# One transformer tower on one core: the first attention's mixing with 128 stationary columns, three divisions, and key slots and a bias moved to other engines

## The reference, cut to what matters

```python
q, k, v = (qkv[:, :, 0], qkv[:, :, 1], qkv[:, :, 2])     # 8 heads, hd = 8
...
scores = jnp.einsum('bhwqd,bhwkd->bhwqk', q, k) * scale
attn = jax.nn.softmax(scores, axis=-1)
out = jnp.einsum('bhwqk,bhwkd->bhwqd', attn, v)          # the mixing
out = out.transpose(0, 2, 3, 1, 4).reshape(B, N, D)
return jnp.einsum('bnd,ed->bne', out, proj_w) + proj_b
...
for n, T in enumerate(NUM_SCALES):                        # second attention
    bias = bias + beta[n] * jnp.cos(two_pi * absdiff / T)
```

## Time and profile before

| | |
|---|---|
| median of 3 runs | 130.06 us (129.52 to 131.12) |
| the profiled execution | 130.09 us |
| its span, first to last instruction | 128.3 us |
| outside the span | 1.8 us |
| instructions | 2347 |
| VectorE, ScalarE, GpSimd busy | 85.2, 62.8, 16.9 us |

### The profile page before, as it was taken

How to read it: one execution, slowest core, us unless ns; L and a number is a source line. 1 busy time by engine, 2 the same in 40 slices (tenths; PEclk the granted TensorE clock), 3 DMA queues, 4 the chain that set the end, 5 groups by cost and what they waited for, 6 DMA issues and landing times.

```text
span 128.3 us, 2347 instructions
## 1 busy us (share of the span) xinstructions
PE 114.1 (89%) x912; PEld 75.3 (59%) x919; DVE 85.2 (66%) x181; ACT 62.8 (49%) x124; POOL 16.9 (13%) x40
## 2 busy tenths in 40 slices
PE   5999999969999989999999996999999999799630
PEld 2334564737687764795686884878768772224330
DVE  0000599799996354558798644487599949999960
ACT  4000668965132175655853647573575646443040
POOL 7300009300000000000022003270013400000000
PEclk9999999999999999999999999999999999999997
DMA  4999980000000000000000000000000000000003
GB/s 156 331 391 432 418 331 2 0 0 0 5 0 3 5 0 0 3 0 5 0 0 0 5 0 0 5 0 0 0 0 0 0 0 3 0 0 5 0 0 82
DMA packets 2682, 6.99 MB, mean 55 GB/s; under 512 B 1264, under 2 KB 1392, under 8 KB 2544
## 3 DMA queue, kind: packets, MB, share of 16 engines
q1 hardware_dynamic: 2672, 6.86, 14.1%
HBM read 6.59 MB, written 0.26 MB: 53 GB/s over the span
## 4 chain that ended last, share of the span: by engine, by line
PE 59%; DVE 17%; DMA 7%; issue 6%; ACT 4%; POOL 2%; SPq 2%; POOLq 1%; ACTq 0%
DMA shared_x<-x_dram 7%; PE PS L395 5%; PE PS L627 5%; PE PS L628 5%; PE PS L309 4%; PE PS L511 3%; PE PS L381 3%; PE PS L635 3%; PE PS L298 3%; PE PS L372 3%; PE PS L497 3%; DVE shared_x L1338 3%; DVE shared_h L1268 2%; PE PS L405 2%; PE PS L317 2%
## 5 line engine op out<-in xcount | busy, mean ns | idle before, releaser
L1268 DVE TENSOR_TENSOR shared_h<-PS,shared_f 128x512 f32<-128x512 f32 x22 | 14.9, 682 | 5.3 <-ACT shared_f L880 5.2
L627 PE MATMUL PS<-xf,up_hi 128*128 128x512 f32 x44 | 17.8, 404 | 0.3 <-DVE shared_h L1268 0.3
L628 PE MATMUL PS<-xf,up_lo 128*128 128x512 f32 x44 | 17.4, 396 | 0.0
L880 ACT ACTIVATE shared_f<-PS 128x512 f32<-128x512 f32 x22 | 12.9, 595 | 7.3 <-PE PS L628 7.3
L279 PE MATMUL PS<-idle_bf 128*128 128x512 bf16 x34 | 10.7, 438 | 1.8 <-POOL idle_bf L911 1.3
L1104 DVE TENSOR_REDUCE top<-PS 128x8 f32<-128x512 f32 x12 | 8.3, 689 | 2.6 <-PE PS L511 1.2
L627 PEld LDWEIGHTS PS<-xf,up_hi 128*128 128x128 f32 x44 | 8.3, 188 | 2.7 <-DVE shared_h L1268 0.9
L1030 DVE TENSOR_SCALAR kf<-PS,pack_a_sb 128x256 f32<-128x256 f32 x1 | 0.5, 484 | 13.4 <-PE PS L287 13.4
L713 ACT ACT_TABLE_LOAD x7 | 9.0, 1283 | 0.8 <-PEq L1463 0.7
L785 ACT ACTIVATE probs<-PS 128x512 f32<-128x512 f32 x8 | 4.8, 597 | 9.3 <-PE PS L381 9.3
L628 PEld LDWEIGHTS PS<-xf,up_lo 128*128 128x128 f32 x44 | 8.3, 188 | 1.8
(11 more groups left out here) (189 smaller groups left out, 217.4 us busy)
## 6 DMA issues: line engine op xcount, KB each, us to landing
shared_x<-x_dram SPq DMA_DIRECT2D x6, 544.0 KB, 6.8
up_w<-pack_d_dram SPq DMA_DIRECT2D x1, 1408.0 KB, 12.5
pack_c_sb<-pack_c_dram SPq DMA_DIRECT2D x1, 796.5 KB, 13.3
pack_b_sb<-pack_b_dram SPq DMA_DIRECT2D x1, 455.0 KB, 9.6
down_w<-pack_e_dram SPq DMA_DIRECT2D x1, 352.0 KB, 13.5
out_dram<-normed SPq DMA_DIRECT2D x4, 64.0 KB, 1.7
pack_a_sb<-pack_a_dram SPq DMA_DIRECT2D x1, 162.0 KB, 9.0
```

Source lines behind the costliest of these rows:

```text
L627: mm(up, up_hi[:, at:at + P], moving, start=True, stop=False)
L628: mm(up, up_lo[:, at:at + P], moving, start=False, stop=True).then_inc(sem("up_mm"), 1)
L880: f(gate[:, n % UPBUF, :], PS[:, UP_BANKS[n % UPBUF][0], :], ACT.Silu).then_inc(sem("gated"), 1)
L1268: v.tensor_tensor(hh[:, ch, :, g * HC:(g + 1) * HC], PS[:, UP_BANKS[n % UPBUF][1], :].rearrange("q (s c) -> q s c", s=2), gate[:, n % UPBU ...
```

## The change

1. The features are sorted to groups and slots in another way (`group_mask`, `slot_mask`, `bq` in `layouts`), so that one slot pair in `probs` holds for both groups' queries the values of heads 4c to 4c+3.
2. `mix1` issues four matmuls in place of eight. The stationary operand has 128 columns (both groups' queries), the moving one 36 (four heads' values and ones). Half of what comes out is of use: each group of 64 partitions has its own two heads in it. Three steps fill a bank, in the banks 4, 5, 4.
3. `divide1` runs three times, for steps 0 to 2, 3 to 5, and 6 and 7: a reciprocal over 48, 48 and 32 values a row, then two multiplications on 64 partitions each, which keep the useful half and write it into `on1`, whose other half a new memset has set to zero. The first stands behind step 5, the others behind step 7.
4. `back1` takes the place of `mixed_to_features` here: the stationary operand is `on1`, 128 partitions by 64 columns, the moving one `fold`, two identities of 64x64 on top of each other (made once by GpSimd), which adds the two groups up.
5. All four key slots of the second half are ScalarE's, two behind the exponential of step 0 and two behind that of step 1; VectorE has none between its steps, and its copies of the second half's values stand behind step 2. ScalarE's copies of values go behind step 2.
6. The bias of the second attention is made by GpSimd in four operations and not by VectorE.

```diff
-        r1 = sb("r1", [P, W8, HEADS])
+        r1 = sb("r1", [P, W8, FH])
+        rec1 = sb("rec1", [P, W8 * 4, 4])
+
+        on1 = shared_h[:, W8 * SLOTS * N:W8 * SLOTS * N + W8 * 2 * D].rearrange("q (w s d) -> q w s d", w=W8, s=2)
+        fold = sb("fold", [P, HALF])
...
+        MIX_BANKS = (4, 5, 4)
...
             def mix1(w):
-                if w % 4 == 0:
-                    pe.wait_ge(sem("v1_act"), w // 4 + 1)
-                    pe.wait_ge(sem("v1_dve"), w // 4 + 1)
+                if w % 3 == 0:
+                    pe.wait_ge(sem("v1_act"), min(w // 3 + 1, 2))
+                    pe.wait_ge(sem("v1_dve"), min(w // 3 + 1, 2))
+                if w == 6:
+                    pe.wait_ge(sem("att1_divided"), 1)
                 pe.wait_ge(sem("att1_probs"), w + 1)
-                wide = 2 * (HD + 1)
+                wide = 4 * (HD + 1)
                 for s in range(2):
-                    r = slice(HALF * s, HALF * s + HALF)
-                    for ch in range(4):
-                        at = ((w % 4) * 4 + ch) * wide
-                        col = (2 * s + ch % 2) * P + (ch // 2) * HALF
-                        t = mm(PS[r, 4 + w // 4, at:at + wide], probs[:, w % 2, col:col + HALF],
-                               vo[:, w % 2, (w // 2) * 2 + s, ch].rearrange("q e d -> q (e d)"), start=True, stop=True)
+                    for pair in range(2):
+                        at = ((w % 3) * 4 + 2 * s + pair) * wide
+                        t = mm(PS[:, MIX_BANKS[w // 3], at:at + wide], probs[:, w % 2, (2 * s + pair) * P:(2 * s + pair + 1) * P],
+                               vo[:, w % 2, (w // 2) * 2 + s, 2 * pair:2 * pair + 2].rearrange("q c e d -> q (c e d)"),
+                               start=True, stop=True)
                 t.then_inc(sem("att1_mixed"), 1)
+
+            def back1(g):
+
+                pe.wait_ge(sem("att1_divided"), g + 2)
+                for w in range(4 * g, 4 * g + 4):
+                    for s in range(2):
+                        t = mm(PS[HALF * s:HALF * s + HALF, g, (w % 4) * N:(w % 4 + 1) * N], on1[:, w, s, :], fold[:, :], start=True, stop=True)
+                t.then_inc(sem("att1_back"), 1)
...
-            mixed_to_features("att1", 0, 0)
+            pe.wait_ge(sem("fold_made"), 1)
+            back1(0)
             mix1(W8 - 1)
             project1(0)
-            mixed_to_features("att1", 1, 1)
+            back1(1)
...
-            between = [last_slot1, values1]
...
-                if w < len(between):
-                    between[w](1)
+                if w == 0:
+                    slots1(1, (0, 1))
+                if w == 1:
+                    slots1(1, (2, 3)).then_inc(sem("k1_act"), 1)
+                if w == 2:
+                    values1(1)
...
+            g_.memset(on1[:, :, :, :], 0.0).then_inc(sem("on1_zeroed"), 1)
...
+            g_.tensor_tensor(fold[:, :], a("ident")[:, 0:HALF], a("ident")[:, HALF:P], ALU.add).then_inc(sem("fold_made"), 1)
...
+            g_.tensor_tensor(bias[:, :], bias[:, :], first_cosine, ALU.add).then_inc(sem("bias_made"), 1)
...
+            def divide1(j):
+
+                blocks = slice(12 * j, min(12 * j + 12, 4 * W8))
+                n = blocks.stop - blocks.start
+                ve.wait_ge(sem("att1_mixed"), blocks.stop // 4)
+                mix = PS[:, MIX_BANKS[j], 0:n * 4 * (HD + 1)].rearrange("q (b e d) -> q b e d", e=4, d=HD + 1)
+                v.reciprocal(rec1[:, blocks], mix[:, :, :, HD]).then_inc(sem("att1_recip"), 1)
+                ve.wait_ge(sem("att1_recip"), j + 1)
+                ve.wait_ge(sem("on1_zeroed"), 1)
+                for h in range(2):
+                    r = slice(HALF * h, HALF * h + HALF)
+                    t = v.tensor_tensor(on1[r].rearrange("q w s (p c e d) -> q (w s p) c e d", p=2, c=2, e=2)[:, blocks, h],
+                                        mix[r, :, 2 * h:2 * h + 2, 0:HD],
+                                        rec1[r, blocks, 2 * h:2 * h + 2].unsqueeze(3).to_broadcast([HALF, n, 2, HD]), ALU.mult)
+                t.then_inc(sem("att1_divided"), 1)
...
-                if w in (1, 2):
-                    first_slots1(1, (range(2), range(2, 3))[w - 1])
-                if w == 3:
+                if w == 2:
                     values1(1)
...
                 if w == 5:
-                    make_bias()
-                if w == 6:
-                    divide("att1", 4, 0, HEADS, HD)
-            divide("att1", 5, 1, HEADS, HD)
+                    divide1(0)
+            divide1(1)
+            divide1(2)
```

More of the change, by code:

```diff
@@ L159, in build @@
         bias = sb("bias", [P, N])
+        first_cosine = shared_h[:, 2 * W8 * SLOTS * N:2 * W8 * SLOTS * N + N]
         q2_bias = sb("q2_bias", [P, 1])
@@ L758, in queries1, with slots1 @@
                 t.then_inc(sem("q1_act"), 1)
-            def last_slot1(g):
+            def slots1(g, slots):
                 act.wait_ge(sem("kf_ready"), g + 1)
-                f(k_slots[:, 4 * g:4 * g + 4, SLOTS - 1, :], half(kf, g).rearrange("q (w n) -> q w n", n=N), ACT.Copy,
-                  scale=b("slot_mask")[:, SLOTS - 1:SLOTS]).then_inc(sem("k1_act"), 1)
+                for h in slots:
+                    t = f(k_slots[:, 4 * g:4 * g + 4, h, :], half(kf, g).rearrange("q (w n) -> q w n", n=N), ACT.Copy,
+                          scale=b("slot_mask")[:, h:h + 1])
+                return t
             def values1(g):
@@ L772, in _ @@
             queries1(0)
-            last_slot1(0)
+            slots1(0, (SLOTS - 1,)).then_inc(sem("k1_act"), 1)
             queries1(1)
@@ L792, in _ @@
             gelus("ffn2", (4, 0))
-            act.wait_ge(sem("bias_made"), 2)
+            act.wait_ge(sem("bias_made"), 1)
             for g in range(2):
@@ L1064, in centre_values2 @@
                 centre("abv", c("abv"), 1).then_inc(sem("v2_centred"), 1)
-            def make_bias():
-                v.tensor_scalar(q2_bias[:, :], c("abq"), float(D) ** -0.5, None, ALU.mult)
-                v.tensor_scalar(bias[:, :], c("cosines")[:, N:2 * N], c("beta")[:, 1:2], None, ALU.mult)\
-                    .then_inc(sem("bias_made"), 1)
-                ve.wait_ge(sem("bias_made"), 1)
-                v.scalar_tensor_tensor(out=bias[:, :], in0=c("cosines")[:, 0:N], scalar=c("beta")[:, 0:1], in1=bias[:, :],
-                                       op0=ALU.mult, op1=ALU.add).then_inc(sem("bias_made"), 1)
             def keys1(g):
@@ L1406, in layouts @@
     feature = np.arange(P)[:, None] % D
+    head = feature // HD
     pack_b = pack(PACK_B, dict(
@@ L1410, in layouts @@
         wq=diag(qkv[0:D].T), wk=diag(qkv[D:2 * D].T), wv=diag(qkv[2 * D:].T), proj=diag(w("L0_tok_proj_w").T),
-        bq=np.where(feature // HD // SLOTS == np.arange(2)[None, :], col(qkv_b[0:D]), np.float32(0)), bk=col(qkv_b[D:2 * D]), bv=col(qkv_b[2 * D:]), bp=col(w("L0_tok_proj_b")),
-        slot_mask=(feature // HD % SLOTS == np.arange(SLOTS)[None, :]).astype(np.float32),
-        group_mask=(feature // HD // SLOTS == np.arange(2)[None, :]).astype(np.float32)))
+        bq=np.where(head // 2 % 2 == np.arange(2)[None, :], col(qkv_b[0:D]), np.float32(0)), bk=col(qkv_b[D:2 * D]), bv=col(qkv_b[2 * D:]), bp=col(w("L0_tok_proj_b")),
+        slot_mask=(head // 4 * 2 + head % 2 == np.arange(SLOTS)[None, :]).astype(np.float32),
+        group_mask=(head // 2 % 2 == np.arange(2)[None, :]).astype(np.float32)))
     n = np.arange(N, dtype=np.float32)
```

10 lines of the change are left out of this document (7 added, 3 removed).

## The result

The changed kernel takes 130.97 us (median of 20 runs, 130.25 to 132.21) against 130.14 us for the kernel before beside it (20 runs, 129.24 to 131.25): a ratio of 1.0073, 95% interval 1.005 to 1.0097. The ratios in this text are taken over the fast runs of both kernels and are not the quotient of the two medians, which is 1.0064 here. The changed kernel is slower by 0.83 us by the medians, inside the 2% that the prediction set as its bound. The forecast of 130.5 us was 0.5 us too low; 130.97 lies inside the range.

The account below looks back on a forecast made before the run. TensorE, busy 89% of the span, was taken to bound the kernel. The terms +0.26 - 0.09 + 0.14 + 0.08 = +0.39 on 130.09 gave 130.48, so 130.5 us, with a range of 129.2 to 131.6.

Parts of the forecast that it names:

- first division stalls the turns of step 6: First attention: VectorE's division behind step 5 exceeds the 0.72 us to spare, so TensorE's turns wait: +0.26 us.
- mixings of steps 5, 6, 7: TensorE behind the stall: dearer wide loads, but no 0.17 us gap before them, so -0.03 us each, -0.09 together.
- last division: On the chain after the last mixing: 0.95 us against 0.81, so +0.14 us.
- ways back: Both `back1` on TensorE's path, with alternating 64-column loads: +0.04 us each, bounds 0 and +0.22, +0.08 together.
- I take 1.11: Length in us taken for VectorE's first division behind step 5, between sums of 1.19 without overlap and 1.03 with it.
- +0.07: Turns of step 6 on TensorE: coming out of a wait they take 0.66 us instead of 0.59.
- ScalarE's slots and GpSimd's bias: Moved key slots have 1.2 us of cover; the bias takes 1.2 us on an idle engine: both cost nothing.
- What follows the attention shifts as a whole: Rest of the kernel behind the attention: a chain of dependent steps, moved as one by the attention's +0.39 us.
- the first: Rival: the mixings' wide loads come faster than the router's 0.111 us; 128.3 to 129.9 us, chance 0.17.
- The second: Rival: half-partition work is dearer, in the divisions' multiplications and the ways back; 131.3 us, to 131.8, chance 0.17.
- The third: Rival: wide loads don't hide behind matmuls, a mixing takes 1.53 us for 0.83; 135.9 us, chance 0.03.
- The fourth: Rival: steps stay at 2.05 us, VectorE absorbs the division, only the tail counts; 130.3 us, chance 0.62 shared with the forecast.

Follow-up runs that it names:

- centre_moved: Changed kernel with the weights' centring behind step 4 split, one part behind step 3, the other behind step 6; 130.74 us, ratio 1.0062 to the kernel before.
- moves: Kernel before with only ScalarE's key slots, the value copies behind step 2 and GpSimd's bias; mixing, divisions, way back as before; 130.16 us, ratio 1.0013.
- fewer_waits: Changed kernel with the wait for the zeroed half of `on1` written once instead of three times; 130.94 us, ratio 1.0078 to the kernel before.
- pad_after: Changed kernel with two dummy one-column memsets at the head of VectorE's stream; 130.84 us, ratio 1.0051 to the kernel before.
- pad_before: Kernel before with two dummy one-column memsets at the head of VectorE's stream; 130.39 us, ratio 1.0009 to the kernel before without them.

## Why the prediction was right, and where its steps were not

Verdict and mechanism hold: a mixing's price is its loads, half as many at 2.5 times the price win next to nothing, and two divisions lie open. The size was 0.4 us short. Term by term, in the attention:

| step of the prediction | forecast | measured |
|---|---|---|
| first division stalls the turns of step 6 | +0.26 | +0.36 |
| idle matmuls | none | -0.11 |
| mixings of steps 5, 6, 7 | 3 x -0.03 | -0.01, -0.01, +0.19 |
| second division | 0 | 0 |
| last division | +0.14 | +0.16 |
| ways back | 2 x 0.04 | 0 |
| sum | +0.39 | +0.58 (+0.56 by the ends) |

*First division.* The step "I take 1.11" was short: start to start it is 37.58 - 36.34 = 1.24. The parts were right (0.45, 2 x 0.36), and the overlap was wrong. The rows that I cited for it give 37.77 + 0.69 - 38.37 = 0.09 and not 0.16; and I subtracted it at the division's end, but the next maximum starts 0.04 behind the last product (36.82 + 0.72 = 37.54), and the overlap in front of the reciprocal was already in its start. The "+0.07" for stalled turns was counted twice: in the sum the turns began with their loads at 38.84, and from there they took 0.66 before as well. Without it the step gives 0.19; with 0.13 for the division and 0.04 for the mixings ahead, which won 0.01 and not 0.03, it gives the 0.36. "centre_moved" shows that this wait is real and can be had back (-0.29). That the division made it, and not something else on VectorE, is read from the trace: 1.24 us stand there in place of 0.54 (37.04 - 36.50), and "moves" without the division has the old stretch.

*Mixings.* "-0.03 for each" failed at step 7. The bargain in a wide mixing is the gap in front of 64-column loads, and that gap is there behind turns: first load 0.31 behind the last of the turns before, 0.11 now. Behind the way back the distance is 0.21 in both kernels, so only the loads count, (7 x 0.111) - (15 x 0.044) = 0.12, and the later end behind the last load (0.06 by the readings of the other mixings): 0.18, measured 0.19. I had the order in front of me, and applied the value of one neighbour to all three. The Trainium skill says, page "TensorEngine Tiling (Array Packing)", section "Key Properties", that a change of mode drains TensorE. This trace agrees at the idle matmuls as well: 128 columns like the wide mixing, and 0.43 for 0.54. It fits behind the way back, too: there the shape changes in both kernels (64*64 to 128*64 before, 128*64 to 128*128 now), and the distance is 0.21 in both, where it is 0.11 between loads of one shape. The same rule that I cited for the mixings I did not apply to what stands behind them, -0.11.

*Ways back.* The alternation that I read from the earlier trace rows holds (16 loads in 0.55), and 64 moving columns cost nothing on top: 0.61 and 0.71 in both chains. The lower bound was right, the value taken was not.

*ScalarE's slots and GpSimd's bias.* Nothing, shown by "moves". ScalarE's two slots took 0.89 and 0.90 in the changed kernel, and no scores waited for them.

*What follows the attention shifts as a whole.* This step failed in the profile: +0.31 and +0.47 came from a stretch whose code is the same. The prediction looked at what each engine computes there, and not at the place that an edit elsewhere gives each instruction in its engine's stream. For the medians the account stays open. 0.56 of the 0.83 us is the attention, since every profile of the changed kernel's stretch reads 21.72 or 21.73. For the 0.3 that is left, the late product and the clock were the candidates, but a kernel in whose profile both are gone ("fewer_waits") is no faster in its median, while "pad_after", in whose profile they cost nothing either, has a ratio lower by 0.003, which the intervals cannot separate. The clock's late fall is not what sets the changed kernel's median. In the profile it takes 0.07 + 3 x 0.50 + 0.14 = 1.71 us of full clock, which is 0.013 of the span, and the mean granted clock over the span is known for every execution: one with 0.988 or more cannot have such a fall. Of the 20 executions of the changed kernel 12 have 0.989 or more, and their median is 130.92, next to 130.97 for all. Whether the late product is in the median stays open; the time up to the first maximum differs by up to 0.5 us between the profiles, which is more than what has to be told apart.

Of the rivals, the first asked for loads below 0.111 us and steps under 1.95; the loads came at (0.97 - 0.19) / 7 = 0.111 and the steps at 2.04. The third is out with them. The second had the multiplications at 0.42 (they took 0.36 for 192 values and 0.30 for 128) and the way back 0.22 dearer. The fourth, a VectorE that absorbs the division, is ruled out by the turns' wait. Two readings were loose without touching the sum: the granted clock is not full in the last slice (7 in the earlier trace rows), and GpSimd's four operations took 0.26 + 0.61 + 0.44 + 0.32 = 1.6 us and not 1.2, still well before they are read.

## What to carry to other kernels

Where small matmuls are bound by their weight loads, read the spacing of loads by shape and by order before cutting their number: here half the loads at 2.5 times the price were worth 0.01 us a mixing, and the same loads in alternating order 0.25. A gap between two groups of matmuls belongs to the pair, so read it for each pair of neighbours. Before work is added to the engine that is second by a little, find the step with room for it, and do not count a stall both in the start and in the length of what it stalls.

## What the hardware showed that I had not expected

- Loads of 128x64 float32 come every (0.80 - 0.14) / 15 = 0.044 us while the outputs stay in one half of the partitions, and every (0.55 - 0.14) / 15 = 0.027 us when they alternate, with the same operands. The Trainium skill, page "TensorE: Matmul & The Clock Gate", section "Part 3: Packing small matmuls — row/col tiling", has loads overlap running matmuls only where the row groups differ; its mechanism also names a background weight buffer. By the row groups the order would not matter: here all loads have the same 128 rows and only the columns' half alternates, and yet the mixing fell from 0.83 to 0.58; the measurement decides. The Trainium skill's page "TensorEngine Tiling (Array Packing)", section "Key Properties", says "Different tiles can execute LdWeights and Matmul in parallel", and that agrees.
- One instruction of VectorE starts 0.21 to 0.29 us later than in the kernel before, relative to what it waits for, in four kernels (the changed one, "centre_moved", "pad_after", "pad_before"). It is number 193 of the stream each time. In the kernel before, number 193 is the reduction behind the last product, which has nothing to wait for, and it comes at once. Two dummies more or two waits fewer in the changed kernel make another product late, or none.
- The granted clock fell to 1.2 GHz for some 3 us behind an idle stretch of 1.46 us in three profiles, not behind 1.45 in a fourth, and not behind 1.23 or 1.24 in the other eight. The fall cost 0.4 to 0.5 us (18.7 to 18.8 from there to the end, where all others have 18.3 to 18.4). At another place it fell in one profile of twelve, behind an idle stretch of 1.21 us that the others have too (1.20 or 1.21), and that fall cost 64.85 - 63.90 = 0.95 us. So the length of the idle stretch alone does not decide it; what else does was not found.
